# Two layers of attention on one core: queries and keys in two float32r parts, scores and maxima in the two row halves of TensorE

## What is computed

```python
# layer 0: one key and value head for all 32 query heads, no mask
attn = softmax(einsum('bnhd,bkd->bhnk', Q, K) / 4)
out  = einsum('bhnk,bkd->bnhd', attn, V) @ Wo + bo      # ffn: silu-gated, 1376 wide
# layer 1: 8 key and value heads, rotary embedding, causal mask
scores = where(causal, einsum('bqhd,bkhd->bhqk', xq, xk) / 4, -inf)
out    = softmax(scores) @ xv @ Wo                      # ffn: base + LoRA, top 2 of 8 experts
```

## Time and profile before

| | us |
|---|---|
| median of 3 runs | 2205.15 (2200.69 to 2208.09) |
| the profiled execution | 2202.45 |
| its span | 2200.7 |
| attention of layer 0 | about 512 to 1293 |
| attention of layer 1 | about 1577 to 2135 |
| mean granted clock | 0.961 |

### The profile page before, as it was taken

One profiled execution on the slowest core, in us unless ns is written; L12 is line 12 of the kernel. 1 busy time (PEld: TensorE's weight loads), 2 busy tenths in 40 slices (PEclk: granted clock), 3 DMA queues, 4 the chain that ended last, 5 costly groups with the idle time before them and its releaser, 6 DMA issues.

```text
span 2200.7 us, 29316 instructions
## 1 busy us (share of the span) xinstructions
PE 2020.8 (92%) x11120; PEld 949.3 (43%) x11120; DVE 1459.4 (66%) x1896; ACT 1102.1 (50%) x2130; POOL 144.8 (7%) x135
## 2 busy tenths in 40 slices
PE   3999999998999999999999986898899999999987
PEld 2878787732222222222222245543433443443436
DVE  7444444437888888888888718339777777777733
ACT  2221211132777777777777742112156666666660
POOL 4000000041000000000000103004200000000010
PEclk7999999997999999999999998999789999999999
DMA  5010100034111112111120121103311211213123
GB/s 172 21 32 12 39 1 0 0 85 106 24 24 27 24 25 43 24 26 25 24 67 19 34 81 52 37 19 98 99 38 32 48 37 35 48 32 80 33 69 118
DMA packets 91747, 99.66 MB, mean 45 GB/s; under 512 B 20033, under 2 KB 71425, under 8 KB 91617
## 3 DMA queue, kind: packets, MB, share of 16 engines
q1 hardware_dynamic: 91616, 97.92, 17.3%
HBM read 69.36 MB, written 27.98 MB: 44 GB/s over the span
## 4 chain that ended last, share of the span: by engine, by line
PE 78%; DVE 14%; DMA 4%; ACT 2%; issue 2%; SPq 1%; POOL 0%; ACTq 0%; DVEq 0%
PE ps L1069 17%; PE ps L1087 16%; PE ps L1051 15%; DVE arena L808 6%; PE ps L869 6%; PE ps L870 6%; PE ps L871 6%; PE ps L987 3%; PE ps L943 3%; DMA arena<-inverse 2%; PE ps L1054 1%; DVE arena L788 1%; ACT arena L607 1%; PE ps L1090 1%; PE ps L934 1%
## 5 line engine op out<-in xcount | busy, mean ns | idle before, releaser
L808 DVE TENSOR_REDUCE arena<-ps 128x1 f32<-128x1024 f32 (+7 forms) x1024 | 976.1, 988 | 261.7 <-PE ps L1054 131.6
L607 ACT ACTIVATE arena<-ps 128x512 f32<-128x512 f32 (+3 forms) x1792 | 892.2, 554 | 389.3 <-PE ps L1087 225.3
L1087 PE MATMUL ps<-arena 98*128 98x512 bf16 (+3 forms) x1792 | 570.0, 361 | 11.0 <-ACT arena L607 6.1
L1051 PE MATMUL ps<-arena 96*128 96x512 bf16 (+3 forms) x1792 | 532.3, 369 | 30.7 <-DVE arena L808 25.1
L1069 PE MATMUL ps<-arena 128*17 128x512 f32 (+3 forms) x3584 | 431.6, 553 | 1.1 <-ACT arena L607 1.1
L1087 PEld LDWEIGHTS ps<-arena 98*128 98x128 bf16 x1792 | 162.5, 97 | 486.3 <-ACT arena L607 372.6
L1051 PEld LDWEIGHTS ps<-arena 96*128 96x128 bf16 x1792 | 163.5, 99 | 214.9 <-DVE arena L808 91.9
L869 PE MATMUL ps<-x_hi,w_hi 128*128 128x512 f32 (+1 forms) x480 | 195.5, 407 | 52.6 <-DVE x_lo L835 31.3
L538 ACT ACTIVATE xn<-ps 128x512 f32<-128x512 f32 (+1 forms) x44 | 26.3, 598 | 275.3 <-PE ps L871 275.3
L870 PE MATMUL ps<-x_lo,w_hi 128*128 128x512 f32 (+1 forms) x352 | 140.5, 399 | 0.0
L871 PE MATMUL ps<-x_hi,w_lo 128*128 128x512 f32 (+1 forms) x352 | 140.2, 398 | 0.0
(11 more groups left out here) (114 smaller groups left out, 1594.6 us busy)
## 6 DMA issues: line engine op xcount, KB each, us to landing
qparts<-arena SPq DMA_DIRECT2D x96, 128.0 KB
arena<-qparts SPq DMA_DIRECT2D x64, 192.0 KB, 3.7
arena<-qparts SPq DMA_DIRECT2D x64, 128.0 KB, 4.0
numer<-arena SPq DMA_DIRECT2D x256, 32.0 KB
xnT<-numer SPq DMA_DIRECT2D x16, 512.0 KB
arena<-inverse SPq DMA_DIRECT2D x16, 512.0 KB
arena<-kparts SPq DMA_DIRECT2D x192, 32.0 KB, 2.9
w_raw<-in_wgu SPq DMA_DIRECT2D x20, 256.0 KB, 3.6
```

What stands on the lines that cost most here:

```text
L607: act.activation(prob[local % P_RING][:, q0:CH], bank(local % SP_RING)[:, q0:CH], ACT.Exp, scale=SCALE).then_inc(S["p_ready"], 1)
L808: dve.tensor_reduce(maxes[c][:, h * TPC + qt:h * TPC + qt + 1], src[:, 0:max_width(l == 1, c, qt)], AX_X, ALU.max).then_inc(S["x_done"], 1)
L1051: last = pe.matmul(dst[:, k0:k1], q_slot[u][0:ROWS, c, h, qt * P:(qt + 1) * P], k_slot[u][0:ROWS, k0:k1], start=True, stop=not diag)
L1087: mm = pe.matmul(bank(slot)[:, q0:CH], k_slot[u][0:ROWS + MROWS, kt * P:(kt + 1) * P], q_slot[u][0:ROWS + MROWS, c, h, q0:CH], start=True, ...
```

## The change

Queries and keys are split into two float32r parts instead of three bf16 parts: 48 rows of products and two maximum rows, 50 in all, which fit a half of the array. Heads 0 and 1 of a group lie in rows 0 to 49, heads 2 and 3 in rows 64 to 113, with the keys in both halves. Every score and maximum matmul names its half by `tile_position`. The order of heads within the maxima is 2, 0, 3, 1. A mask is two matmuls of 64 rows instead of one of 128. The pace is given piece by piece; in layer 0 ten items of a group are left to the group itself, in layer 1 none but the transpose; the transpose of the second chunk comes two items into the next group's maxima. The maximum rows are four DMAs instead of two. There are three slots instead of four, each of 12 DMAs as before, in 4-byte elements. The high part is made by ScalarE, the low one by VectorE, and POOL's subtraction is gone; POOL fills three whole key slots with ones instead of two rows of four. In the projection TensorE waits tile by tile instead of chunk by chunk. In the last group all items left have step 0. POOL makes nine selects of identity and masks instead of three.

```diff
-SLOTS = 4
-ITERS = B * NG // SLOTS
+SLOTS = 3
...
-MID_LAG = 2
-PARTS = 3
-ROWS = 6 * DH
+HI_LAG = 2
+PARTS = 2
+ROWS = 3 * DH
 MROWS = 2
+HALF = P // 2
 XN_RING = [8, TT]
 NX = TPC * HG
-XI = NX + 1
-MAX_END = [0.98, 0.95]
-TAIL = [11, 0]
+MAX_END = [1.0, 0.95]
+AHEAD = [6, NX]
...
+def row0(h):
+
+    return HALF * (h // 2)
+
+
+def max_blocks():
+
+    heads = (2, 0, 3, 1)
+    blocks = []
+    for n in range(B * NG):
+        r = [[(n, c, qt, h) for qt in range(TPC) for h in heads] for c in range(QC)]
+        before = [(n - 1, 1, None, None)] if n else []
+        blocks.append(r[0][:2] + before + r[0][2:] + r[1][:2] + [(n, 0, None, None)] + r[1][2:])
+    blocks[-1].append((B * NG - 1, 1, None, None))
+    return blocks
...
-                for row, rows in ((0, 3 * DH), (3 * DH, 2 * DH), (5 * DH, DH)):
+                for t in range(2):
+                    r = HALF * t
+                    qh = q[2 * t:2 * t + 2, :, :]
                     for c in range(QC):
-                        sp.dma_start(q_slot[u][row:row + rows, c, :, :],
-                                     q[:, 0:rows, c * CH:(c + 1) * CH].rearrange("h r q -> r h q")).then_inc(S["slot_in"][u], 16)
-                for row, s in ((0, 0), (1, 0), (2, 0), (3, 1), (4, 1), (5, 2)):
-                    sp.dma_start(k_slot[u][row * DH:(row + 1) * DH, :],
-                                 k[:, s * DH:(s + 1) * DH, :].rearrange("o d q -> (o d) q")).then_inc(S["slot_in"][u], 16)
+                        cols = slice(c * CH, (c + 1) * CH)
+                        sp.dma_start(q_slot[u][r:r + DH, c, :, :],
+                                     qh[:, 0:DH, cols].rearrange("h r q -> r h q")).then_inc(S["slot_in"][u], 16)
+                        sp.dma_start(q_slot[u][r + DH:r + 3 * DH, c, :, :],
+                                     qh[:, :, cols].rearrange("h r q -> r h q")).then_inc(S["slot_in"][u], 16)
+                    sp.dma_start(k_slot[u][r:r + 2 * DH, :], k.rearrange("o d q -> (o d) q")).then_inc(S["slot_in"][u], 16)
+                    sp.dma_start(k_slot[u][r + 2 * DH:r + 3 * DH, :],
+                                 k[:, 0:DH, :].rearrange("o d q -> (o d) q")).then_inc(S["slot_in"][u], 16)
...
-                for s in range(MROWS):
-                    sp.dma_start(q_slot[u][ROWS + s:ROWS + s + 1, c, :, :].rearrange("o h (t q) -> o (h t) q", q=P),
-                                 negm[c][0:NX, s, :]).then_inc(S["m_in"][c], 16)
-
-            def store_o(l, it, u, c):
-                S = L[l]
-                n = it * SLOTS + u
+                for t in range(2):
+                    for s in range(MROWS):
+                        r = HALF * t + ROWS + s
+                        sp.dma_start(q_slot[u][r:r + 1, c, :, :].rearrange("o h (t q) -> o (h t) q", q=P),
+                                     negm[c][t * NX // 2:(t + 1) * NX // 2, s, :].bitcast(F32)).then_inc(S["m_in"][c], 16)
...
+                sp.wait_ge(S["v_slot_ready"], SLOTS)
...
+                    if n + SLOTS - 1 < GROUPS:
                         sp.wait_ge(S["pv_done"], n * group_quads[l] + PQ)
-                        load_slot(l, it if u == 0 else it + 1, v)
-                    if TAIL[l]:
-                        max_rows(l, u, 1, n * QC + 1)
-                        store_o(l, it, u, 0)
+                        load_slot(l, n + SLOTS - 1)
+                    max_rows(l, u, 1, n * QC + 1)
+                    store_o(l, n, 0)
                     if not final:
-                        max_rows(l, (u + 1) % SLOTS, 0, (n + 1) * QC)
...
+                        max_rows(l, v, 0, (n + 1) * QC)
+                    store_o(l, n, 1)
...
-                for c in range(NCH):
-                    for m in range(NQ):
-                        rows = DH if (m == KC and l == 0) else P
-                        pool.wait_ge(S["mid_done"], c * NQ + m + 1)
-                        pool.tensor_tensor(part[m][0:rows, 2, :], rest[m][0:rows, :], part[m][0:rows, 1, :],
-                                           ALU.subtract).then_inc(S["lo_done"], 1)
-                    if c == 0:
-                        pool.wait_ge(S["lo_done"], NQ)
-                        for u in range(SLOTS):
-                            pool.memset(k_slot[u][ROWS:ROWS + MROWS, :], 1.0).then_inc(S["v_slot_ready"], 1)
-                        pool.wait_ge(S["v_slot_ready"], SLOTS)
+                pool.wait_ge(S["lo_done"], NQ)
+                for u in range(SLOTS):
+                    pool.tensor_copy(k_slot[u].bitcast(F32R), v_all[:, 0, 0, DH:DH + 1].to_broadcast([P, N])).then_inc(S["v_slot_ready"], 1)
+                pool.wait_ge(S["v_slot_ready"], SLOTS)
...
-                def middle(i):
...
-                    act.wait_ge(S["rest_ready"], i + 1)
-                    act.activation(part[m][0:rows, 1, :], rest[m][0:rows, :], ACT.Copy).then_inc(S["mid_done"], 1)
...
-                        act.wait_ge(S["q_ready"], i + 1)
+                    if c:
+                        act.wait_ge(S["q_out"][m], c * (16 * PARTS))
+                    act.activation(part[m][0:rows, 0, :], src[0:rows, :], ACT.Identity, bias=bias).then_inc(S["hi_done"], 1)
+
+                def high_roped(i):
+                    act.wait_ge(S["rope_done"], i + 1)
+                    high(i, q32[i % NQ], 0.0)
+
+                for i in range(NCH * NQ):
+                    c, m = divmod(i, NQ)
+                    rows = 2 * DH if (m == KC and l == 0) else P
+                    if c:
+                        act.wait_ge(S["lo_done"], i - NQ + 1)
+                    act.wait_ge(S["q_ready"], i + 1)
+                    if l == 0:
+                        bias = bias_q[:, m:m + 1] if m < KC else bias_kv[:, 0:1]
+                        high(i, bank(m), bias if m < KC else bias_kv[0:DH, 0:1])
                         act.activation(q32[m][0:rows, :], bank(m)[0:rows, :], ACT.Identity, bias=bias).then_inc(S["q32_ready"], 1)
-                        if i >= MID_LAG:
-                            middle(i - MID_LAG)
+                    else:
+                        act.activation(q32[m], bank(m), ACT.Copy).then_inc(S["q32_ready"], 1)
+                        if i >= HI_LAG:
+                            high_roped(i - HI_LAG)
+                for i in range(NCH * NQ - HI_LAG if l else NCH * NQ, NCH * NQ):
+                    high_roped(i)
...
+                def rope(i):
+
+                    c, m = divmod(i, NQ)
                     pos = slice(c % QC * CH, (c % QC + 1) * CH)
-                    for m in range(NQ):
-                        rows = DH if (m == KC and l == 0) else P
-                        dve.wait_ge(S["q32_ready"], c * NQ + m + 1)
-                        if c:
-                            dve.wait_ge(S["q_out"][m], c * (16 * PARTS))
-                        if l:
-
-                            dve.stream_shuffle(rest[m], q32[m], swap).then_inc(dve_chain, 1)
-                            made[0] += 1
-                            dve.wait_ge(dve_chain, made[0])
-                            dve.tensor_tensor(q32[m], q32[m], rope_cos[:, pos], ALU.mult).then_inc(dve_chain, 1)
-                            dve.tensor_tensor(rest[m], rest[m], rope_sin[:, pos], ALU.mult).then_inc(dve_chain, 1)
-                            made[0] += 2
-                            dve.wait_ge(dve_chain, made[0])
-                            dve.tensor_tensor(q32[m], q32[m], rest[m], ALU.add).then_inc(dve_chain, 1)
-                            made[0] += 1
-                            dve.wait_ge(dve_chain, made[0])
-                        dve.tensor_copy(part[m][0:rows, 0, :], q32[m][0:rows, :]).then_inc(S["hi_done"], 1)
-                        dve.wait_ge(S["hi_done"], c * NQ + m + 1)
-                        dve.tensor_tensor(rest[m][0:rows, :], q32[m][0:rows, :], part[m][0:rows, 0, :], ALU.subtract).then_inc(S["rest_ready"], 1)
-                        if l == 0 and c and m == 0:
-                            take_v(c - 1)
+                    dve.wait_ge(S["q32_ready"], i + 1)
+                    chained(dve.stream_shuffle(rest[m], q32[m], swap))
+                    wait_chain()
+                    chained(dve.tensor_tensor(q32[m], q32[m], rope_cos[:, pos], ALU.mult))
+                    chained(dve.tensor_tensor(rest[m], rest[m], rope_sin[:, pos], ALU.mult))
+                    wait_chain()
+                    dve.tensor_tensor(q32[m], q32[m], rest[m], ALU.add).then_inc(S["rope_done"], 1)
+
+                def lower(i):
+
+                    m = i % NQ
+                    rows = DH if (m == KC and l == 0) else P
+                    dve.wait_ge(S["hi_done"], i + 1)
+                    dve.wait_ge(S["rope_done"] if l else S["q32_ready"], i + 1)
+                    dve.tensor_tensor(part[m][0:rows, 1, :], q32[m][0:rows, :], part[m][0:rows, 0, :].bitcast(F32),
+                                      ALU.subtract).then_inc(S["lo_done"], 1)
+
+                for i in range(NCH * NQ):
+                    if l:
```

(85 more changed lines are left out.)

239 lines of the change are left out of this document (102 added, 137 removed).

## The result

The changed kernel takes 2548.01 us (median of 4 runs, 2537.54 to 2569.34) against 2202.92 before: ratio 1.158, 95% interval 1.150 to 1.165. The forecast was 2333, range 2225 to 2455. The sign was right, and the size was missed by 215 us.

What follows compares the result with a forecast made beforehand. TensorE was taken as the bound, VectorE close behind in layer 0; after the change, a loop through the P·V quad. Terms -2 + 3 + 100 - 3 + 12 - 20 + 33 + 5 = +128 on 2202.45 gave 2330, as median 2333; range 2225 to 2455.

Steps and rivals of the forecast that it cites:

- The lap of layer 0: Layer 0's attention: a lap goes from 2.83 to 3.26 us, a group from 47.0 to 53.7, +100 in all.
- S3: Layer 0's lap: the score issued right behind the P·V quad, ahead of the maximum's second piece; quad to S3 put at 0.98 us.
- the 0.18: Layer 0's lap: exposed weight loads of S3 and the second piece behind it, 0.09 us each, between independent and queued loading.
- The 3.17 a lap: Layer 0's lap without the queued load's 0.09 us, if matmuls in different row groups start about 4 ns apart.
- What is next to be late: Layer 0, after the loop through the quad: ScalarE, from laps without maxima at 2.38 us.
- rival (a): Faster: the reduce sets the pace, layer 0 at 39.3 us a group, layer 1 about 27.5, total about 2000; chance 0.06.
- The last group of layer 0: All ten maxima and the transpose stand behind its first score: about 54.5 us for about 42.5, +12 (+9 to +16).
- up to 3 us until the clock is back: Layer 0's last group: allowance for the clock's return after scores halt 13.7 us, beside 63 scores at 2.38 per four.
- Layer 1's projection: VectorE sets it; without POOL's subtraction and a cast a tile needs at most 3.45 us: -20 (-17 to -22).
- Layer 1's attention: From 33.3 to 35.5 us a group (32.5 to 39.9): +33, and +5 for opening and last group.
- Rival (c): The clock stays low because TensorE waits in each lap of layer 0: 85 us a group, total 2805; chance 0.13.
- Rival (b): Halves don't overlap in float32r, or loads serialise wholly: 55.9 and 39.9 us a group, total about 2443; chance 0.12.

Runs made afterwards that it cites:

- the filler: Changed kernel plus overwritten 384-column bf16 matmuls on the score's own 64 rows, ahead of every score of layer 1's attention and layer 0's last group: 2479.20 us.
- one due time: Changed kernel with both pieces of a maximum given the same due time, so that no piece pair is divided: 2549.98 us.
- no masks: Changed kernel with the causal masks of layer 1 left out and nothing in their place: 2545.32 us.

## Why the prediction was right in layer 0 and wrong in size

- **The lap of layer 0** is right: 3.25 us for 3.26 and 53.2 us a group for 53.7. Taken from start to start, as the prediction took them, its terms came out one by one: first piece to quad 0.42 (653.02 to 653.44) for 0.09 + 0.31, quad to S3 0.98 (653.44 to 654.42), S3 to reduce 0.57 (654.42 to 654.99) for 0.18 + 0.42. That the loads queue up, which the 0.18 assumed, did not show: those of both halves start at 654.42. The rule of the Trainium skill (TensorE: Matmul & The Clock Gate, Part 3: Packing small matmuls) on starts in different row groups agrees with 642.69 twice. The 3.17 a lap that I drew from it was further off than 3.26.
- **What is next to be late** was wrong. I named ScalarE at 2.38 us a lap from the earlier trace rows; with the division gone it is the ring of score banks at 2.83. It would also have stopped rival (a), the reduce setting the pace, which I refused for another reason.
- **The last group of layer 0**, +12, was +38. The step that failed is "up to 3 us until the clock is back": it fell at 1354 and was still at 0.50 when the last quad went out at 1429.9. No row had given those 3 us. I had taken, laps without maxima at 2.38 us, as what such laps do, but those are laps of 98 rows.
- **Layer 1's projection**, -20, gave -15. A tile takes 3.31 us on VectorE for at most 3.45, and POOL is out; the difference is at the end, where ScalarE's last copies wait until stores of the chunk before have left their tiles, and the piece below of 7.29 us is such a store (chain of the changed kernel):

```profile
1646.52 0.63 DVE arena L796
...
1649.83 0.62 DVE arena L796
...
1678.80 7.29 DMA kparts<-arena
```

- **Layer 1's attention** is where the forecast went wrong: +38 in the sum, about +220 on the chip (10 + 167 + 43). The step that failed is the price of 35.5 us a group, "nearer the middle than either": it was a price at the full clock, nothing in the working says so, and the bounds of 32.5 and 39.9 were prices at the full clock too. The runs show 46.2 us at a mean clock of 0.69 in its place. As a price at the full clock 35.5 is not refuted: 37.4 with the filler bounds it from above, and by estimate 46.2 x 0.69 = 31.9 and 43.5 x 0.80 = 34.8 us of full-clock work and waits lie about it.
- **Rival (c)** had the cause and the wrong place. It looked for the low clock where TensorE would wait, in the laps of layer 0, and argued from waits and unbroken stretches. Layer 0 waits most (busy 46.17 of 53.20 us) and kept 1.00 but for short falls and its last group; layer 1 hardly waits (567 of 601) and lost it. With 0.13 it was too small, and layer 1 had no case of its own, though the row of 12 us at 0.50 with PE busy 10.30 in the earlier trace rows already shows a busy engine at the low clock. The stated range counted only the costs of instructions.
- **Rival (b)**, halves that don't overlap, is refused by the common starts; its 55.9 us a group was also too low: 57.8 at the best, and with the clock gone much more.

## What to carry to other kernels

When a change makes matmuls narrower in rows, price its stretches at both clocks and ask which one each will have; in these runs the rows at work and the matmuls side by side kept it up, and the share of busy time in the profile didn't tell. Where a list of due times is cut finer, look at what now stands between two parts that a third engine needs together. And read an experiment by stretches: two of these (one due time, no masks) changed the total by under 3 us while both causes moved by many times that.

## What the runs showed that I had not expected

- Halving the rows of bf16 matmuls, with columns and instructions kept, took the clock from 1.00 to 0.50 and the kernel from 2203 to 3389 us.
- Putting 14 idle rows of each half to work, with ones, raised the clock of layer 1 from 0.69 to 0.80 and took 66 us off.
- Matmuls on all rows among matmuls in halves are dear: twelve more a group took layer 1 from 46.2 to 63.9 us a group, and 64 masks on 128 rows in place of 128 on 64 took it to 79.2.
- Why the stretches in halves of layer 1 swing between the two clocks group by group, and differ a little from kernel to kernel, stays open. So does what the element type does to the clock.
